# Reordering four engines' queues in a gated recurrent layer: `bw` before `yT`, `xc` before the last `M`, exponentials before squares, `ce` before `sqa`

## The chip, the core and the metric

One NeuronCore of a Trainium2 chip runs the whole kernel. Its engines are TensorE (PE in the profile, with its weight loads as PEld), VectorE (DVE), ScalarE (ACT), GpSimd (POOL) and SyncE (SP, which here issues DMAs). Each engine works through its own queue in order and waits on semaphores. The metric is the device time of one execution in microseconds, the median of several.

## The reference

The layer normalises u (4 sequences of 1024 tokens, 128 channels), runs a recurrent block with 32 heads, state 64 x 64 per head, and multiplies its output by a gate. Cut to what matters:

```python
proj = u @ in_proj_w.T                       # z, x, B, C, dt, theta, lambda
Bm = _rms(Braw, B_norm_w)[:, :, None, :] + B_bias
Cm = _rms(Craw, C_norm_w)[:, :, None, :] + C_bias
tc = jnp.cumsum(theta, axis=1)               # angles; rope() rotates B and C by them
Bm, Cm = rope(Bm), rope(Cm)
...
h = a_t * h + g_t * Bx + b_t * prevBx        # Bx = outer(x_t, B_t), scan over t
y = einsum('bhpn,bhn->bhp', h, C_t)
...
y = (y + xh * D) * silu(z)
y = _rms(y, norm_w)
return y @ out_proj_w.T
...
return x + s * silu(ffn(xn))                 # s: the block's output, ffn in emulated fp8
```

## The kernel before

A first part (`prepare`, about the first 145 us) normalises the input, transposes weights and stores tables to DRAM. The rest, `units`, is a loop over 8 super-tiles t of 512 tokens (four chunks of 128; two super-tiles make a sequence) and, inside, over 8 groups q of four heads: 64 units. The recurrence is done in chunks. In each chunk the outputs are a masked product of scores (C times B, in `s`) with decays (`E`), called `M`, applied to x (`xk`), plus the state (`hs`, `k_carry`) applied to decayed C (`ce`). There is no scheduler: every queue is in the order in which the code is written, and the queues are software-pipelined by hand. While a unit's outputs are formed, the next unit's B and C are rotated.

The names in one unit, with the engine that writes them:

- VectorE: `part` (L1299, eight of 128x512, products of B or C with rows of sines and cosines `k_trig`; both tensors are in SBUF), `ang` (L1274, angle subtraction), `hs` and `k_carry` (L1363, L1373, states), `xc` (L1283, two, x scaled for the skip, from PSUM), `M` (L1317, four, decay matrices from PSUM scores and `E`), `yT` (L1409, two, gated outputs, from PSUM), `bw` (L1309, two, B scaled by decays, from PSUM).
- GpSimd: `rot` (L1524, four, sum of two `part`), `ce` (L1533, two, decayed C), `sqa` (L1568, two, running sum of squares of the outputs over a super-tile; one, L1561, where q=0). All read and write SBUF.
- ScalarE: `E` (L1455, exponentials of `d`), `xk` (L1460, copies of x), `sz` (L1502), the sines `k_tri`, `sq` (L1465, squares of `yT`), and `rnd` (L1440, rounding for `ang`).
- TensorE: x products into `r` (L1112, `x_by_token`), whose result ScalarE copies and VectorE scales; transposes of rotated B into `r` (L1118), `d`, `s`, `y`, the output projection `o`, and at q=0 the column sums of `sqa` of the previous super-tile (L1164, `square_sums`), for the root mean square.
- SyncE copies the sines to both halves of the partitions (`k_trig`, eight DMAs a unit, L74) and loads the decay rows `eb` for `ce`, which it may overwrite once `ce` of the unit before is done.

Two waits matter at the places that the change touches. In TensorE's queue, at q=0, the sum of squares stands ahead of the x products of the next unit:

```python
                    exponents(t, q, 3)
                    if q == 0 and t > 0:
                        square_sums(t - 1)
                    if live(t, q + 1):
                        ...
                        x_by_token(t, q + 1, 0)
```

and it waits for the last `sqa` of the super-tile before (`pe.wait_ge(sqa_ready, at(T2, t, T2))`, L1162). In VectorE's queue each `xc` waits for ScalarE's copy of the same x (`x_copied`, L1279).

Of the kernel before, what the change touches and what calls it, by code (L numbers as in the profile page):

```python
# [36 lines left out]
NQ = H // 4  # L37
# [870 lines left out]
def units(nc, K, u, scratch, cum_stored, logs_stored, bc_loaded, xn_loaded, out):  # L908

    xn_d, tc_d, bc_d, cum_d, cumt_d, gate_d, logs_d, ecum_d = scratch  # L910
    with ExitStack() as ctx:
# [67 lines left out]
        def at(per, t, k):  # L979

            return t * per + max(k, 0) + 1
# [5 lines left out]
        def begins(t):  # L990

            return t % SPB == 0

        def ends(t):

            return t % SPB == SPB - 1
# [5 lines left out]
        def live(t, q):  # L1002

            return t * NQ + q < NS * NQ
# [260 lines left out]
        def _(dve):  # L1265
# [89 lines left out]
            for t in range(NS):  # L1355
                def state(t, q, c):

                    into = 1
                    if c == 0:
                        dve.wait_ge(y_ready, at(T2, t, 2 * q))  # L1360
                        dve.wait_ge(st_ready, at(T1, t, q + 1))
                        if begins(t):
                            nc.vector.tensor_copy(hs[:, 0, :, :].rearrange("n p d -> n (p d)"), R[1][:, 0:2 * HD]).then_inc(hch, 2)  # L1363
                            return
                    if c == CS - 1 and ends(t):
                        return
                    if c == CS - 2 and ends(t):
                        into = 2
                    dve.wait_ge(hch, at(T8, t, 8 * q + 2 * c))
                    for p in range(2):  # L1370
                        src = before(t, q, c, p)
                        dst = hs[:, c, p, :] if c < CS - 1 else K["carry"][:, t % 2, 2 * q + p, :]
                        nc.vector.scalar_tensor_tensor(  # L1373
                            out=dst, in0=src, scalar=K["dtot"][:, (t * CS + c) * NP + 2 * q + p:(t * CS + c) * NP + 2 * q + p + 1],
                            in1=R[1][:, (2 * c + p) * 64:(2 * c + p) * 64 + 64], op0=ALU.mult, op1=ALU.add).then_inc(hch, into)

                for q in range(NQ):
                    tn = t if q < NQ - 1 else t + 1
                    if live(t, q + 1):
                        rotation(t, q + 1, 0, 0, 0)  # L1380
                    if live(t, q + 2):
                        angles(t, q + 2)
                    for c in range(CS):
                        state(t, q, c)
                    if live(t, q + 1):
                        rotation(t, q + 1, 0, 0, 1)
                        x_scaled(t, q + 1, tn, 0)
                    scores(t, q, 2)
                    scores(t, q, 3)
                    if q == 0 and t > 0:  # L1390
                        norm_start(t - 1)
                    if live(t, q + 1):
                        x_scaled(t, q + 1, tn, 1)
                    if live(t, q + 1):
                        for p, w in ((1, 0), (0, 1), (1, 1)):
                            rotation(t, q + 1, p, w, 0)
                            rotation(t, q + 1, p, w, 1)
                            if q == 0 and t > 0:
                                if w == 0:
                                    norm_seeded(t - 1)  # L1400
                                else:
                                    norm_refined(t - 1, p)

                    for p in range(2):
                        dve.wait_ge(sz_ready, at(T2, t, 2 * q + p + 1))
                        dve.wait_ge(y_ready, at(T2, t, 2 * q + p + 1))
                        dve.wait_ge(out_ready, at(T1, t, q))
                        dve.wait_ge(sq_ready, at(T2, t, 2 * q))
                        nc.vector.tensor_tensor(yT[:, p, :], Yp[p][:], sz[:, p, :], ALU.mult).then_inc(yt_ready, 1)  # L1409
                    if q == 0 and t > 0:  # L1410
                        norm_refined(t - 1, 2)
                    if live(t, q + 1):
                        b_decayed(t, q + 1, tn)
                    if live(t, q + 1):
                        scores(t, q + 1, 0)
                        scores(t, q + 1, 1)
# [13 lines left out]
        def _(act):  # L1430
# [55 lines left out]
            for t in range(NS):  # L1486
                for q in range(NQ):
                    if live(t, q + 2):
                        rounding(t, q + 2)
                    decays(t, q, 2)  # L1490
                    decays(t, q, 3)
                    if q == 1 and t > 0:
                        normalised(t - 1)
                    if live(t, q + 1):
                        x_copy(t, q + 1, 0)
                        x_copy(t, q + 1, 1)
                    if q == 0 and t > 0:
                        root(t - 1)
                    for p in range(2):
                        act.wait_ge(z_ready, at(T2, t, 2 * q + p + 1))  # L1500
                        act.wait_ge(yt_ready, at(T2, t, 2 * q - 1 + p))
                        nc.scalar.activation(sz[:, p, :], R[p][:], ACT.Silu).then_inc(sz_ready, 1)  # L1502
                    if live(t, q + 2):
                        sines(t, q + 2)
                    if live(t, q + 1):
                        decays(t, q + 1, 0)
                    squares(t, q, 0)
                    if live(t, q + 1):
                        decays(t, q + 1, 1)
                    squares(t, q, 1)  # L1510
            root(NS - 1)
            normalised(NS - 1)
# [1 line left out]
        @block.gpsimd  # L1514
        def _(pool):
            for s in (rot_ready, ce_ready, sqa_ready):
                pool.sem_inc(s, 1)

            def sums(t, q, k):

                w, p = k // 2, k % 2
                pool.wait_ge(part_ready, at(T8, t, 8 * q + 2 * k + 2))
                pool.wait_ge(y_ready, at(T2, t, 2 * q - 2))
                nc.gpsimd.tensor_tensor(rot[:, q % 2, p, w, :], part[:, 2 * p, :], part[:, 2 * p + 1, :],  # L1524
                                        ALU.add).then_inc(rot_ready, 1)

            def c_decayed(t, q):

                pool.wait_ge(eb_loaded, 32 * (t * NQ + q + 1))
                for p in range(2):  # L1530
                    pool.wait_ge(rot_ready, at(T4, t, 4 * q + 4))
                    pool.wait_ge(y_ready, at(T2, t, 2 * q - 1 + p))
                    nc.gpsimd.tensor_tensor(ce[:, p, :], rot[:, q % 2, p, 1, :], eb[:, p, :], ALU.mult).then_inc(ce_ready, 1)  # L1533

            def gated_out(t):

                pool.wait_ge(acc_done, at(1, t, 1))
                pool.wait_ge(gate_loaded, 16 * (t + 1))
                nc.gpsimd.tensor_tensor(so[:], so[:], gate[:], ALU.mult).then_inc(gated, 1)

            def finished(t):

                pool.wait_ge(gated, t + 1)
                pool.wait_ge(res_loaded, 16 * (t + 1))
                nc.gpsimd.tensor_tensor(res[:], so[:], res[:], ALU.add).then_inc(o_ready, 1)

            for k in range(4):
                sums(0, 0, k)
            for t in range(NS):
                for q in range(NQ):  # L1550
                    c_decayed(t, q)
                    if live(t, q + 1):
                        for k in range(4):
                            sums(t, q + 1, k)
                            if k == 0 and q == 2 and t > 0:
                                gated_out(t - 1)
                            if k == 0 and q == 3 and t > 0:
                                finished(t - 1)
                    if q == 0:
                        pool.wait_ge(sq_ready, at(T2, t, 2))  # L1560
                        nc.gpsimd.tensor_tensor(sqa[:], sq[:, 0, :], sq[:, 1, :], ALU.add).then_inc(sqa_ready, 1)  # L1561
                        pool.wait_ge(sqa_ready, at(T2, t, 1))
                        pool.sem_inc(sqa_ready, 1)  # L1563
                        continue
                    for p in range(2):
                        pool.wait_ge(sq_ready, at(T2, t, 2 * q + p + 1))
                        pool.wait_ge(sqa_ready, at(T2, t, 2 * q + p))
                        nc.gpsimd.tensor_tensor(sqa[:], sqa[:], sq[:, p, :], ALU.add).then_inc(sqa_ready, 1)  # L1568
# [42 lines left out]
```

## Time and profile before

| | |
|---|---|
| median of 3 runs | 1208.13 us (1207.28 to 1209.54) |
| the profiled execution | 1207.62 us, span 1205.7 us |
| granted TensorE clock, mean | 0.971 |
| VectorE busy | 1144.0 us (95%) |
| TensorE busy | 1124.8 us (93%) |
| ScalarE busy | 819.0 us (68%) |
| GpSimd busy | 755.5 us (63%) |

Busy shares are of the span of the profiled execution. GpSimd's and ScalarE's rows leave room; VectorE's and TensorE's hardly do, though a TensorE that is shown busy needn't be at its peak. From about 150 us on the granted clock is in its top tenth.

### The profile page before, as it was taken

The numbers are of one execution on the slowest core, as the hardware profiler recorded it, in microseconds if no ns is written. First come the engines' busy times: TensorE is split into PE (matmuls) and PEld (weight loads), VectorE is DVE, ScalarE is ACT, GpSimd is POOL, SyncE is SP. The second block draws the span as 40 slices with busy tenths as digits, with TensorE's granted clock in tenths as the row PEclk, the third lists the DMA queues.
The fourth block names the chain that finished last, engine by engine and source line by source line (L and its number), as shares of the span: only waits on it lengthen the run. The fifth ranks groups of instructions, "written<-read, shape, count | busy, mean of one in ns | idle before, by whom it ended". The sixth has DMA issues, their size and how long they took to land.

```text
span 1205.7 us, 30426 instructions
## 1 busy us (share of the span) xinstructions
PE 1124.8 (93%) x11442; PEld 817.4 (68%) x11442; DVE 1144.0 (95%) x1821; ACT 819.0 (68%) x1270; POOL 755.5 (63%) x560
## 2 busy tenths in 40 slices
PE   3878399999999999999999999999999999999996
PEld 3663267777777767777776777776777777777775
DVE  7899599999999999999999999999999999999994
ACT  4678366677676677667667776667767767777663
POOL 5000247776776767666776677776767687667774
PEclk9976699999999999999999999999999999999999
DMA  8654555544645465546555464546444655444450
GB/s 180 219 148 104 124 113 119 113 106 103 144 106 125 103 142 117 118 98 137 116 124 107 94 148 112 122 104 152 105 116 99 136 117 128 107 90 98 113 118 16
DMA packets 91888, 142.94 MB, mean 119 GB/s; under 512 B 19326, under 2 KB 38591, under 8 KB 91327
## 3 DMA queue, kind: packets, MB, share of 16 engines
q1 hardware_dynamic: 91743, 141.00, 50.5%
q8 instruction: 91, 1.49, 0.6%
q14 instruction: 54, 0.44, 0.1%
HBM read 58.68 MB, written 13.37 MB: 60 GB/s over the span
## 4 chain that ended last, share of the span: by engine, by line
PE 59%; DVE 17%; issue 7%; DMA 2%; ACT 1%; SPq 1%; POOL 0%; DVEq 0%; POOLq 0%; ACTq 0%
PE y L1235 10%; PE r L1221 8%; PE s L1138 7%; PE o L1153 6%; PE r L1112 5%; PE y L1229 5%; PE r L1118 5%; PE y L1245 5%; DVE hs L1373 3%; DVE M L1317 3%; DVE bw L1309 3%; PE r L1107 3%; DVE xc L1283 3%; PE r L1193 3%; PE d L1127 3%
## 5 line engine op out<-in xcount | busy, mean ns | idle before, releaser
L1524 POOL TENSOR_TENSOR rot<-part 128x512 f32<-128x512 f32 x256 | 384.1, 1500 | 315.9 <-DVE part L1299 315.9
L1299 DVE SCALAR_TENSOR_TENSOR part<-k_bcs,k_prmT,k_trig 128x512 f32<-128x512 f32 x512 | 524.8, 1072 | 13.5 <-issue 9.7
L1455 ACT ACTIVATE E<-d 128x512 f32<-128x512 f32 x256 | 152.9, 597 | 184.5 <-PE d L1127 184.2
L1533 POOL TENSOR_TENSOR ce<-rot,eb 128x512 f32<-128x512 f32 x128 | 185.8, 1471 | 2.3 <-POOLq L1563 2.1
L1317 DVE TENSOR_TENSOR M<-s,E 128x512 f32<-128x512 f32 x256 | 163.3, 676 | 2.0 <-PE s L1138 1.6
L1568 POOL TENSOR_TENSOR sqa<-sqa,sq 128x512 f32<-128x512 f32 x112 | 142.7, 1274 | 31.3 <-ACT sq L1465 22.7
L1112 PE MATMUL r<-k_w_zx,k_xns 128*128 128x256 f32 x512 | 137.0, 391 | 13.6 <-issue 9.4
L1138 PE MATMUL s<-rot 64*128 64x128 f32 x2048 | 149.4, 286 | 0.0
L1138 PEld LDWEIGHTS s<-rot 64*128 64x128 f32 x2048 | 124.9, 188 | 35.2 <-issue 34.8
L1460 ACT COPY xk<-r 128x512 f32<-128x512 f32 x128 | 75.3, 588 | 106.8 <-PE r L1112 106.6
L1235 PE MATMUL y<-M,xk 128*64 128x128 f32 x2048 | 140.1, 279 | 0.0
L1153 PEld LDWEIGHTS o<-k_w_o,yT 128*128 128x128 f32 x1024 | 132.8, 192 | 8.5 <-DVE yT L1409 1.7
L1221 PE MATMUL r<-k_xns,k_w_zx 128*128 128x512 f32 x256 | 133.2, 614 | 3.8 <-DVE xc L1283 1.8
L1153 PE MATMUL o<-k_w_o,yT 128*128 128x128 f32 x1024 | 133.4, 275 | 1.4 <-DVE yT L1409 1.4
L1235 PEld LDWEIGHTS y<-M,xk 128*64 128x64 f32 x2048 | 109.2, 136 | 21.5 <-issue 21.5
L1112 PEld LDWEIGHTS r<-k_w_zx,k_xns 128*128 128x128 f32 x512 | 90.5, 192 | 31.9 <-issue 11.0
L1127 PE MATMUL d<-k_cum,k_pick 123*128 123x512 bf16 x256 | 99.4, 388 | 0.0
L1502 ACT ACTIVATE sz<-r 128x512 f32<-128x512 f32 x128 | 75.7, 597 | 32.7 <-PE r L1221 32.1
L1283 DVE TENSOR_TENSOR xc<-r,k_cc 128x512 f32<-128x512 f32 x128 | 87.0, 680 | 4.8 <-ACT xk L1460 4.7
L1193 PEld LDWEIGHTS r<-xk,bw 128*64 128x64 f32 x1792 | 57.5, 137 | 48.8 <-DVE bw L1309 48.0
L1229 PEld LDWEIGHTS y<-k_ident,xc 128*128 128x128 f32 x512 | 58.8, 140 | 44.7 <-issue 44.7
L1409 DVE TENSOR_TENSOR yT<-y,sz 128x512 f32<-128x512 f32 x128 | 81.6, 676 | 6.3 <-PE y L1245 6.3
(253 smaller groups left out, 1676.3 us busy)
## 6 DMA issues: line engine op xcount, KB each, us to landing
k_trig<-k_tri SPq DMA_DIRECT2D x512, 128.0 KB, 2.4
eb<-ecum_rows SPq DMA_DIRECT2D x128, 256.0 KB, 4.7
k_bcs<-bc_t SPq DMA_DIRECT2D x16, 256.0 KB, 4.1
k_bcs<-bc_t SPq DMA_DIRECT2D x32, 128.0 KB, 4.2
k_bcs<-in_L_attn_u SPq DMA_DIRECT2D x4, 512.0 KB, 6.1
xn_t<-a_xnT SPq DMA_DIRECT2D x1, 2048.0 KB, 11.5
tc_t<-a_tcT SPq DMA_DIRECT2D x1, 2048.0 KB, 15.9
bc_t<-a_tmp SPq DMA_DIRECT2D x1, 2048.0 KB, 8.5
```

Source lines behind the costliest of these rows:

```text
L1112: last = nc.tensor.matmul(R[i][:, 256 * c:256 * c + 256], xns[:, (t + q // NQ) % 2, (2 * i + c) * P:(2 * i + c + 1) * P], K["w_zx"][:, DI ...
L1127: nc.tensor.matmul(Dp[:], K["pick"][:, head * P:head * P + P], K["cum"][0:D_ROWS, q % 2, h, :], start=True, stop=True).then_inc(d_ready, 1)
L1138: last = nc.tensor.matmul(Sp[j][:, k], rot[rows, q % 2, p, 0, k], rot[rows, q % 2, p, 1, k], start=True, stop=True)
L1153: last = nc.tensor.matmul(Op[:, k], yT[:, p, k], K["w_o"][:, (2 * q + p) * P:(2 * q + p + 1) * P], start=False, stop=q == NQ - 1 and c == ...
L1221: nc.tensor.matmul(R[p][:], w, xns[:, t % 2, :], start=True, stop=True).then_inc(z_ready, 1)
L1235: nc.tensor.matmul(Yp[p][m:m + 64, k], xk[:, par, c, 128 * p + m:128 * p + m + 64], M[:, 2 * p + j, k], start=False, stop=c == 0 and begin ...
L1299: nc.vector.scalar_tensor_tensor(out=part[:, 2 * p + f, :], in0=bcs[:, (t + q // NQ) % 2, 2 * w + f, :], scalar=col, in1=trig[:, p, 1 - f, ...
L1317: nc.vector.tensor_tensor(M[:, h, :], Sp[h % 2][:], E[:, h % 2, :], ALU.mult).then_inc(m_ready, 1)
L1455: nc.scalar.activation(E[:, h % 2, :], Dp[:], ACT.Exp).then_inc(e_ready, 1)
L1524: nc.gpsimd.tensor_tensor(rot[:, q % 2, p, w, :], part[:, 2 * p, :], part[:, 2 * p + 1, :], ALU.add).then_inc(rot_ready, 1)
L1533: nc.gpsimd.tensor_tensor(ce[:, p, :], rot[:, q % 2, p, 1, :], eb[:, p, :], ALU.mult).then_inc(ce_ready, 1)
L1568: nc.gpsimd.tensor_tensor(sqa[:], sqa[:], sq[:, p, :], ALU.add).then_inc(sqa_ready, 1)
```

## The change

Four queues get another order; the instructions and their operands stay.

- VectorE scales B for the next unit (`bw`) ahead of the gated outputs `yT`, and the second `xc` ahead of the unit's last `M`.
- ScalarE computes the second exponential of the next unit ahead of the first of the two squares.
- GpSimd computes the decayed C of the next unit (`ce`) at the end of the iteration before, after its four `rot` and ahead of that iteration's `sqa`.

```diff
                     scores(t, q, 2)
-                    scores(t, q, 3)
                     if q == 0 and t > 0:
                         norm_start(t - 1)
                     if live(t, q + 1):
                         x_scaled(t, q + 1, tn, 1)
+                    scores(t, q, 3)
...
+                    if live(t, q + 1):
+                        b_decayed(t, q + 1, tn)
                     for p in range(2):
                         dve.wait_ge(sz_ready, at(T2, t, 2 * q + p + 1))
...
                     if q == 0 and t > 0:
                         norm_refined(t - 1, 2)
-                    if live(t, q + 1):
-                        b_decayed(t, q + 1, tn)
...
                         decays(t, q + 1, 0)
+                        decays(t, q + 1, 1)
                     squares(t, q, 0)
-                    if live(t, q + 1):
-                        decays(t, q + 1, 1)
                     squares(t, q, 1)
...
             for k in range(4):
                 sums(0, 0, k)
+            c_decayed(0, 0)
             for t in range(NS):
                 for q in range(NQ):
-                    c_decayed(t, q)
                     if live(t, q + 1):
                         for k in range(4):
                             sums(t, q + 1, k)
...
+                        c_decayed(*((t, q + 1) if q < NQ - 1 else (t + 1, 0)))
                     if q == 0:
```

GpSimd's queue from the end of one super-tile into the next. Before (`sqa` with one input, L1561, is the first of a super-tile, after its q=0):

```order
L1524 TENSOR_TENSOR rot<-part 128x512 x4
L1568 TENSOR_TENSOR sqa<-sqa,sq 128x512 x2
L1533 TENSOR_TENSOR ce<-rot,eb 128x512 x2
L1524 TENSOR_TENSOR rot<-part 128x512 x4
L1561 TENSOR_TENSOR sqa<-sq 128x512
```

and the same stretch of the changed kernel:

```order
L1523 TENSOR_TENSOR rot<-part 128x512 x4
L1532 TENSOR_TENSOR ce<-rot,eb 128x512 x2
L1568 TENSOR_TENSOR sqa<-sqa,sq 128x512 x2
L1523 TENSOR_TENSOR rot<-part 128x512 x4
L1532 TENSOR_TENSOR ce<-rot,eb 128x512 x2
L1561 TENSOR_TENSOR sqa<-sq 128x512
```

The pair of `ce` has moved ahead of the pair of `sqa`, for which TensorE waits at this place.

VectorE's queue from the second `part` of a unit with q=0 into the next unit (`nrm` and `tch` are small steps of the root mean square). Before:

```order
L1299 SCALAR_TENSOR_TENSOR part<-k_bcs,k_prmT,k_trig 128x512
L1283 TENSOR_TENSOR xc<-r,k_cc 128x512
L1317 TENSOR_TENSOR M<-s,E 128x512 x2
L1323 TENSOR_SCALAR nrm<-y 128x4
L1283 TENSOR_TENSOR xc<-r,k_cc 128x512
...
L1338 SCALAR_TENSOR_TENSOR tch<-tch,nrm 128x4
L1409 TENSOR_TENSOR yT<-y,sz 128x512 x2
L1342 SCALAR_TENSOR_TENSOR nrm<-tch,nrm 128x4
L1309 TENSOR_TENSOR bw<-r,k_dec 128x512 x2
L1317 TENSOR_TENSOR M<-s,E 128x512 x2
```

and in the changed kernel:

```order
L1299 SCALAR_TENSOR_TENSOR part<-k_bcs,k_prmT,k_trig 128x512
L1283 TENSOR_TENSOR xc<-r,k_cc 128x512
L1317 TENSOR_TENSOR M<-s,E 128x512
L1323 TENSOR_SCALAR nrm<-y 128x4
L1283 TENSOR_TENSOR xc<-r,k_cc 128x512
L1317 TENSOR_TENSOR M<-s,E 128x512
...
L1338 SCALAR_TENSOR_TENSOR tch<-tch,nrm 128x4
L1309 TENSOR_TENSOR bw<-r,k_dec 128x512 x2
L1411 TENSOR_TENSOR yT<-y,sz 128x512 x2
L1342 SCALAR_TENSOR_TENSOR nrm<-tch,nrm 128x4
L1317 TENSOR_TENSOR M<-s,E 128x512 x2
```

Of the four `M` of a unit the last one has moved behind the second `xc`, and the two `bw` ahead of the two `yT`.

## Rows read from the trace of the kernel before

**Rows 1.** The page, part 1: busy time of VectorE.
```profile
PE 1124.8 (93%) x11442; PEld 817.4 (68%) x11442; DVE 1144.0 (95%) x1821; ACT 819.0 (68%) x1270; POOL 755.5 (63%) x560
```

**Rows 2.** Sorted waits: engine and line, waited for, total us, times, longest.
```profile
POOL rot L1524 <- DVE part L1299: 315.9, 256, 41.7
...
PEld r L1221 <- DVE xc L1283: 50.5, 63, 1.5
...
DVE part L1299 <- DMA k_trig<-k_tri: 3.2, 9, 0.5
```

**Rows 3.** Timeline of VectorE, t=3 q=6: start us, duration us, engine, line.
```profile
641.07 1.27 DVE L1409 TENSOR_TENSOR yT<-y,sz 128x512 f32<-128x512 f32 x2
642.27 1.27 DVE L1309 TENSOR_TENSOR bw<-r,k_dec 128x512 f32<-128x512 f32 x2
...
644.66 1.46 DVE L1299 SCALAR_TENSOR_TENSOR part<-k_bcs,k_prmT,k_trig 128x512 f32<-128x512 f32 x1
...
648.11 0.93 DVE L1299 SCALAR_TENSOR_TENSOR part<-k_bcs,k_prmT,k_trig 128x512 f32<-128x512 f32 x1
...
650.76 0.67 DVE L1283 TENSOR_TENSOR xc<-r,k_cc 128x512 f32<-128x512 f32 x1
651.36 6.09 DVE L1299 SCALAR_TENSOR_TENSOR part<-k_bcs,k_prmT,k_trig 128x512 f32<-128x512 f32 x6
```

**Rows 4.** Timeline of GpSimd in the same unit.
```profile
641.23 1.27 POOL L1524 TENSOR_TENSOR rot<-part 128x512 f32<-128x512 f32 x1 [0.63 <-DVE part L1299]
...
642.89 2.69 POOL L1568 TENSOR_TENSOR sqa<-sqa,sq 128x512 f32<-128x512 f32 x2 [0.39 <-ACT sq L1465]
...
645.54 2.96 POOL L1533 TENSOR_TENSOR ce<-rot,eb 128x512 f32<-128x512 f32 x2
```

**Rows 5.** Timeline of TensorE and ScalarE in the same unit.
```profile
646.78 1.13 PE L1112 MATMUL r<-k_w_zx,k_xns 128*128 128x256 f32 x4
...
649.70 0.59 ACT L1460 COPY xk<-r 128x512 f32<-128x512 f32 x1 [1.17 <-PE r L1112]
...
656.65 1.09 PE L1118 MATMUL r<-k_ident,rot 128*128 128x128 f32 x8
```

**Rows 6.** Timeline of VectorE in an even super-tile, t=4 q=6.
```profile
771.93 1.27 DVE L1409 TENSOR_TENSOR yT<-y,sz 128x512 f32<-128x512 f32 x2
...
779.00 0.75 DVE L1299 SCALAR_TENSOR_TENSOR part<-k_bcs,k_prmT,k_trig 128x512 f32<-128x512 f32 x1
...
782.06 6.10 DVE L1299 SCALAR_TENSOR_TENSOR part<-k_bcs,k_prmT,k_trig 128x512 f32<-128x512 f32 x6
```

**Rows 7.** Timeline of the boundary units, t=4 q=0, then t=5 q=0.
```profile
673.67 1.27 DVE L1409 TENSOR_TENSOR yT<-y,sz 128x512 f32<-128x512 f32 x2
...
679.38 0.95 PE L1164 MATMUL y<-k_ones,sqa 128*128 128x1 f32 x8
...
804.24 1.27 DVE L1409 TENSOR_TENSOR yT<-y,sz 128x512 f32<-128x512 f32 x2
...
809.71 0.95 PE L1164 MATMUL y<-k_ones,sqa 128*128 128x1 f32 x8
...
812.29 0.69 DVE L1283 TENSOR_TENSOR xc<-r,k_cc 128x512 f32<-128x512 f32 x1 [0.30 <-ACT xk L1460]
...
813.43 0.59 ACT L1460 COPY xk<-r 128x512 f32<-128x512 f32 x1 [1.17 <-PE r L1112]
...
814.76 1.40 DVE L1299 SCALAR_TENSOR_TENSOR part<-k_bcs,k_prmT,k_trig 128x512 f32<-128x512 f32 x2
```

**Rows 8.** Timeline of VectorE, t=4 q=1, then t=5 q=1.
```profile
690.66 1.27 DVE L1409 TENSOR_TENSOR yT<-y,sz 128x512 f32<-128x512 f32 x2
...
701.21 6.10 DVE L1299 SCALAR_TENSOR_TENSOR part<-k_bcs,k_prmT,k_trig 128x512 f32<-128x512 f32 x6
...
820.99 1.27 DVE L1409 TENSOR_TENSOR yT<-y,sz 128x512 f32<-128x512 f32 x2
...
831.31 6.10 DVE L1299 SCALAR_TENSOR_TENSOR part<-k_bcs,k_prmT,k_trig 128x512 f32<-128x512 f32 x6
```

## The prediction, made before the changed kernel had run

> **What bounds the kernel now.** I read the page first: VectorE is busy for 1144.0 of 1205.7 us [rows 1]. The sorted waits come next. Their largest entries are other engines waiting for VectorE: GpSimd waits 315.9 us for rotation products, and TensorE's loads wait 50.5 us for `xc` [rows 2]. VectorE itself has almost no idle time, so in the main loop the time is VectorE's time, and only what shortens or interrupts its row counts.
>
> Then the timeline of one ordinary unit (t=3, q=6). I count offsets from its first gated output `yT`, 641.07 in the trace. VectorE has two `yT` and two `bw` (0.60 apart each), two `M`, the first `part` at 3.59, the angle subtraction, the states, the second `part` at 7.04, `xc`, two `M`, `xc` at 9.69, and six `part` from 10.29 that end at 16.38 [rows 3]. Every row starts 0.08 before its predecessor's end, so the unit is 16.30 long. Its counterpart in an even super-tile has the six products at 10.13 and is 16.15 long [rows 6].
>
> The reader should look at how long `part` takes. It reads two SBUF tensors, as every GpSimd addition and product here does. Six take 6.09 us, yet the second one of the even unit takes 0.75 [rows 3, 6]. The first one of the ordinary unit takes 1.46. It starts at 3.59 while GpSimd's pair of `sqa` runs from 1.82 to 4.51, and it ends at 5.05, 0.54 after the pair [rows 3, 4]. The second takes 0.93 and ends at 7.97, 0.54 after GpSimd's `ce` pair (7.43). GpSimd waits likewise: its `ce` pair takes 2.96, against 2.50 for two products of 1.27 overlapped by 0.04. So the two engines exclude each other for whole instructions, and at a hand-over the waiting VectorE product goes first. An `M`, `yT`, `bw` or `xc` with one input in PSUM isn't lengthened. What remains of VectorE's loss in the first 10 us of a unit is thus the placing of two `part` against GpSimd's two pairs.
>
> [...]
>
> **The change, part by part.** No instruction is added or removed on any engine; each keeps its duration.
>
> *`bw` ahead of `yT`.* Swapping two pairs of equal length moves nothing behind them on VectorE. `bw` needs the transposes of B, which run on TensorE from 656.65 to 657.74, while VectorE would ask for the first at 657.37 and the second at 657.97 [rows 5]. The first four of eight transposes are done by then, so there's no wait now, with some 0.1 to spare, and more where TensorE runs ahead. Cost 0. `yT` comes 1.20 later. Who waits: ScalarE's squares, now also behind the second exponential (below).
>
> *Exponential ahead of squares.* ScalarE's squares end about 0.6 later; their reader `sqa` stands behind `ce` now, so this is hidden. The cover is `ce`, which ends at 4.07, against squares done near 3.2. The rounding behind them ends near 3.9, before the angle subtraction wants it at 4.54. Cost 0.
>
> *`ce` ahead of `sqa`.* The last `rot` ends at 1.43 [rows 4]. `ce` follows 0.14 later (the gap inside the dependent `sqa` pair: 2.69 less two times 1.27 is 0.15) and ends at 1.57 + 2.50 = 4.07. The first `part` starts at 3.59 as before, is blocked to 4.07 and ends at 4.62 rather than 5.05: 0.43 won. The `sqa` pair comes behind it. In the rows before, a pair ends 2.38 after the product that held it (645.54 + 2.96 against 644.66 + 1.46), and the dependence adds 0.18: 4.62 + 2.56 = 7.17. The second `part` starts 1.99 after the first's end, at 6.61, inside this pair, and ends at 7.17 + 0.54 = 7.72 rather than 7.97. So 0.25 is left of the 0.43. In an even unit the second `part` starts at 7.07 at the latest, also before 7.17, and ends at 7.72 rather than 7.82: 0.10 [rows 6].
>
> *`xc` ahead of the last `M`.* VectorE would start the second `xc` at 7.72 - 0.08 + 1.20 = 8.84 instead of 9.69. It needs ScalarE's copy, which ends at 9.22 now; that chain starts with TensorE's x product at 5.71, released by the angle subtraction [rows 5]. Released 0.43 earlier, the copy ends at 8.79: just in time, by 0.05. TensorE gets `xc` earlier, but TensorE isn't the bound. Gain 0, bounds 0 and 0.4 lost per unit.
>
> An ordinary unit thus loses 0.25 (odd t) or 0.10 (even t). There are 19 and 20 of q = 3 to 7: 19 x 0.25 + 20 x 0.10 = 6.8 us won. Lower bound 0 (the copy late by what was won), upper bound 0.43 each, 17 us.
>
> *The boundary between super-tiles.* At q=0, t>0 TensorE's sum of squares (L1164) waits for the last `sqa` of the previous super-tile, and everything behind it on TensorE's queue waits too: both x products, then the copies, both `xc`. Now it starts at 809.71, 5.47 into the unit (5.71 in an even one), long after `sqa`'s end [rows 7]. Afterwards `sqa` ends at 7.17, so it starts at 7.27 (0.1 for the signal, estimated from the 0.08 between a `part` end and its `rot`). That is 1.80 (1.56) later. From there the second copy ends 4.31 later (813.43 + 0.59), `xc` at 4.34. Before, the six products came at 5.05 after the sums, since both `M` had filled the wait; now the last `M` stands behind `xc`, so they come 4.34 + 0.60 + 0.60 = 5.54 after. Cost of a boundary: 1.80 + 0.49 = 2.29 (odd), 2.05 (even); 4 x 2.29 + 3 x 2.05 = 15.3 us over seven.
>
> *The two units after it.* In q=1 there is a single `sqa`, which ends near 5.7, so the second `part` isn't blocked; TensorE starts its scores 0.4 earlier and the copies come near 7.5 and 8.4. The six products start at about 9.93, not 10.32 (odd) or 10.55 (even) [rows 8]: 4 x 0.39 + 3 x 0.62 = 3.4 us won. In q=2 TensorE is late after a short q=1, and `bw` waits up to 0.4 for its transposes; I take no change there (bounds 0.5 won, 0.9 lost).
>
> **Sum.** +15.3 - 3.4 - 6.8 = +5.1 us. The profiled execution took 1207.62 us (span 1205.7 and 1.9 around it), 0.5 under the median of 1208.13. So 1212.7 us, 0.38% above the median. What a measurement of this kernel can tell from no change is about 0.2%, 2.4 us.
>
> **Rivals.** *No change to be measured.* The ordinary units save 0.1 more each, by TensorE's lead over its `bw` and `xc` waits: 46 units, 4.6 us, 1208. Against it: VectorE has no wait in those rows that this lead could shorten.
>
> *Faster.* The sum of squares isn't held. If GpSimd got through `sqa` by 5.5, the seven boundaries would cost nothing and 10.2 us stay won: 1197.4. The point is 10.2 / 7 = 1.46 per boundary; below it the change gains. For it: `sqa` is only 2.7 us of work. Against: the `ce` pair alone fills GpSimd to 4.07, and even with the first `part` not in between `sqa` would end at 6.7, 1.2 too late.
>
> *Slower still.* The first `part` arrives after 4.03 instead of 3.59. Then `sqa` takes over directly from `ce`, and `part` waits until 5.3 and ends near 5.9; a unit loses about 0.9 instead of winning. What could delay it: a late `bw` in q=2, or the trig rows, whose landing already holds `part` nine times, by up to 0.5 us [rows 2]. Seven to fifteen such units give 1219 to 1226.
>
> **How the numbers follow.** My forecast 0.60 (own range 1209 to 1217), no change 0.17, faster 0.13, slower still 0.10. The range reaches to 1203, into the faster case, and to 1219, and leaves out what lies beyond 1219 and below 1203, about 2 in 10. A part of the forecast's range lies under 1210.5. So: faster by over 0.2% 0.17, within 0.19, slower 0.64.
>
> **What would show it.** Right: the L1164 sums start near 7.3 into their unit and VectorE's first `xc` there waits about 2 us, seven times; in an ordinary unit the first `part` takes about 1.0 and the second about 1.1, and the unit is 16.05; `sqa` runs from 4.6 to 7.2. Wrong: boundary units of 17 us; or first products of 1.5 us and more; or waits of VectorE for the transposes or for the copies (`bw`, `xc`) in ordinary units, which would mean that TensorE, not the exclusion, sets the new period.

## The result and the profile after

The changed kernel takes 1235.2 us (median, 1234.1 to 1235.62), the kernel before 1208.31 in the same comparison: a ratio of 1.0207, 95% interval 1.018 to 1.0233. The profiled execution took 1234.1 us, 26.5 more than that of before. The sign was forecast, the size wasn't: 1212.7 was predicted, with 1219 as the upper end.

The page of the kernel after, busy time of each engine and the granted clock in 40 slices:

```profile
PE 1120.3 (91%) x11442; PEld 830.5 (67%) x11442; DVE 1144.4 (93%) x1821; ACT 814.2 (66%) x1270; POOL 755.1 (61%) x560
...
PEclk9976699999999999998999999999999999999999
```

VectorE's busy time is the same as in [rows 1] to 0.4 us, and a product that GpSimd holds up counts as busy, so nearly all of the 26.5 us is idle time on VectorE. The sorted waits say where (engine and line, waited for, total us, times, longest):

```profile
DVE xc L1283 <- ACT xk L1460: 31.3, 20, 4.0
...
PE y L1164 <- POOL sqa L1568: 15.5, 8, 2.1
...
DVE bw L1309 <- PE r L1118: 5.5, 9, 2.6
```

The reader should see that two of the three rows belong together. TensorE waits 15.5 us for `sqa`, at most 2.1 us at a time (seven boundaries and once after the last unit), and VectorE then waits 31.3 us for the x copies, up to 4.0 us at a time. A wait of 2.1 has become one of 4.0 further down.

An ordinary unit, t=3 q=6, the same as in [rows 3 to 5] (timeline: start us, duration us, engine, line):

```profile
652.98 1.28 DVE L1309 TENSOR_TENSOR bw<-r,k_dec 128x512 f32<-128x512 f32 x2
...
654.54 2.52 POOL L1532 TENSOR_TENSOR ce<-rot,eb 128x512 f32<-128x512 f32 x2
...
656.57 1.03 DVE L1299 SCALAR_TENSOR_TENSOR part<-k_bcs,k_prmT,k_trig 128x512 f32<-128x512 f32 x1
...
657.01 3.14 POOL L1568 TENSOR_TENSOR sqa<-sqa,sq 128x512 f32<-128x512 f32 x2
...
659.59 1.11 DVE L1299 SCALAR_TENSOR_TENSOR part<-k_bcs,k_prmT,k_trig 128x512 f32<-128x512 f32 x1
...
661.18 0.59 ACT L1460 COPY xk<-r 128x512 f32<-128x512 f32 x1 [1.17 <-PE r L1112]
...
661.82 0.68 DVE L1283 TENSOR_TENSOR xc<-r,k_cc 128x512 f32<-128x512 f32 x1
...
663.02 6.09 DVE L1299 SCALAR_TENSOR_TENSOR part<-k_bcs,k_prmT,k_trig 128x512 f32<-128x512 f32 x6
```

It goes as worked out. The first `part` starts at 3.59 and takes 1.03 instead of 1.46, the second takes 1.11 inside `sqa`, the copy ends 0.05 before `xc` starts, and the six products come at 10.04. The unit is 16.05 long.

The boundary of t=5 (`yT` of this unit follows `bw` at 819.14, so offsets count from there), as in [rows 7]:

```profile
826.44 1.02 PE L1164 MATMUL y<-k_ones,sqa 128*128 128x1 f32 x8 [2.09 <-POOL sqa L1568]
...
827.33 1.31 PE L1112 MATMUL r<-k_w_zx,k_xns 128*128 128x256 f32 x4
828.43 1.92 PE L1153 MATMUL o<-k_w_o,yT 128*128 128x128 f32 x8
...
829.29 0.69 DVE L1283 TENSOR_TENSOR xc<-r,k_cc 128x512 f32<-128x512 f32 x1 [2.45 <-ACT xk L1460]
...
830.14 1.71 PE L1112 MATMUL r<-k_w_zx,k_xns 128*128 128x256 f32 x4
...
832.51 0.69 DVE L1283 TENSOR_TENSOR xc<-r,k_cc 128x512 f32<-128x512 f32 x1 [1.85 <-ACT xk L1460]
...
833.71 1.41 DVE L1299 SCALAR_TENSOR_TENSOR part<-k_bcs,k_prmT,k_trig 128x512 f32<-128x512 f32 x2
```

The sums start at 7.30, where 7.27 was forecast. But the second four x matmuls take 1.71 and the projection between them 1.92; at the boundary of t=4 and in the ordinary unit the same instructions take 1.03 and 1.05. Three stretches behind the start of the sums of this boundary (start, end and length of the stretch; then busy us and instruction count of PE, PEld, DVE, ACT and POOL; the third figure from the end is the granted clock):

```profile
826.40:828.10 1.70, 1.66 (x12) 1.61 (x13) 0.44 (x1) 0.00 (x0) 1.18 (x1) 1.00 0.53 157
828.10:831.52 3.42, 3.42 (x14) 3.06 (x13) 1.36 (x3) 0.59 (x1) 0.09 (x1) 0.50 0.00 1
831.52:833.50 1.98, 1.98 (x13) 1.47 (x12) 0.99 (x2) 1.59 (x2) 0.00 (x0) 1.00 0.00 0
```

TensorE had been idle for 2.09 us before the sums, and behind them its granted clock is 0.50 for 3.4 us: 1.2 GHz instead of 2.4. The boundary of t=4 had the same wait and kept its clock:

```profile
692.40:694.10 1.70, 1.65 (x12) 1.60 (x13) 0.45 (x1) 0.00 (x0) 1.17 (x1) 1.00 0.94 165
694.10:697.50 3.40, 3.40 (x24) 2.90 (x22) 2.00 (x5) 1.83 (x3) 0.10 (x1) 1.00 0.04 9
...
694.28 1.05 PE L1153 MATMUL o<-k_w_o,yT 128*128 128x128 f32 x8
695.17 1.03 PE L1112 MATMUL r<-k_w_zx,k_xns 128*128 128x256 f32 x4
```

In 3.4 us of the same queue it gets through 24 matmul instructions there, against 14 above.

Measured from the end of one unit's eighth `part` to the next, and summed by q over both traces, the difference is this:

| units | before, us | after, us | difference | forecast |
|---|---|---|---|---|
| boundaries, q=0 of t=1 to 7 | 117.45 | 144.54 | +27.1 | +15.3 |
| q=1 of t=1 to 7 | 115.61 | 117.05 | +1.4 | -3.4 |
| q=2, all t | 132.11 | 136.10 | +4.0 | 0 |
| q=3 to 7, 39 units | 632.46 | 626.92 | -5.5 | -6.8 |

The boundary of t=4, with the full clock, took 19.08 us, the six others, each with a stretch at 0.50, 20.5 to 22.1.

### The profile page after: what moved, and what is told of

Read it like the earlier page. It is cut to its first block and busy times, and to the rows that moved or that the text cites. A ratio compares the mean times of both kernels' runs of the same rounds, so it can differ in the third digit from the quotient of the medians.

```text
span 1232.2 us, 30426 instructions
## 1 busy us (share of the span) xinstructions
PE 1120.3 (91%) x11442; PEld 830.5 (67%) x11442; DVE 1144.4 (93%) x1821; ACT 814.2 (66%) x1270; POOL 755.1 (61%) x560
## 5 line engine op out<-in xcount | busy, mean ns | idle before, releaser
L1568 POOL TENSOR_TENSOR sqa<-sqa,sq 128x512 f32<-128x512 f32 x112 | 165.7, 1480 | 15.6 <-ACT sq L1465 7.6
L1317 DVE TENSOR_TENSOR M<-s,E 128x512 f32<-128x512 f32 x256 | 168.4, 677 | 1.8 <-PE s L1138 1.5
L1532 POOL TENSOR_TENSOR ce<-rot,eb 128x512 f32<-128x512 f32 x128 | 161.1, 1281 | 8.5
L1112 PE MATMUL r<-k_w_zx,k_xns 128*128 128x256 f32 x512 | 145.4, 409 | 22.9 <-issue 9.3
L1138 PE MATMUL s<-rot 64*128 64x128 f32 x2048 | 149.3, 285 | 16.9 <-DVE M L1317 16.9
L1153 PEld LDWEIGHTS o<-k_w_o,yT 128*128 128x128 f32 x1024 | 138.1, 198 | 9.2 <-DVE yT L1411 1.7
L1153 PE MATMUL o<-k_w_o,yT 128*128 128x128 f32 x1024 | 138.4, 281 | 1.4 <-DVE yT L1411 1.4
L1221 PE MATMUL r<-k_xns,k_w_zx 128*128 128x512 f32 x256 | 121.1, 594 | 0.5 <-DVE xc L1283 0.4
L1283 DVE TENSOR_TENSOR xc<-r,k_cc 128x512 f32<-128x512 f32 x128 | 87.3, 682 | 31.5 <-ACT xk L1460 31.3
L1502 ACT ACTIVATE sz<-r 128x512 f32<-128x512 f32 x128 | 75.7, 597 | 17.3 <-PE r L1221 11.5
## 6 DMA issues: line engine op xcount, KB each, us to landing
tc_t<-a_tcT SPq DMA_DIRECT2D x1, 2048.0 KB, 16.3
```

The source lines that it names most:

```text
L1112: last = nc.tensor.matmul(R[i][:, 256 * c:256 * c + 256], xns[:, (t + q // NQ) % 2, (2 * i + c) * P:(2 * i + c + 1) * P], K["w_zx"][:, DI ...
L1138: last = nc.tensor.matmul(Sp[j][:, k], rot[rows, q % 2, p, 0, k], rot[rows, q % 2, p, 1, k], start=True, stop=True)
L1153: last = nc.tensor.matmul(Op[:, k], yT[:, p, k], K["w_o"][:, (2 * q + p) * P:(2 * q + p + 1) * P], start=False, stop=q == NQ - 1 and c == ...
L1221: nc.tensor.matmul(R[p][:], w, xns[:, t % 2, :], start=True, stop=True).then_inc(z_ready, 1)
L1317: nc.vector.tensor_tensor(M[:, h, :], Sp[h % 2][:], E[:, h % 2, :], ALU.mult).then_inc(m_ready, 1)
```

## The experiments

The quoted text in each part is what was expected before its run. The unit times below are measured in the same way, each in one profiled execution. Ratios are to the kernel before in the same comparison. In the traces of the experiments the stage ahead of the loop took about 147 us or, in three of them, about 154; the kernel before, whose times there lie near 1208 and near 1215, seems to do the same. This widens the medians by some 6 us. The unit times don't contain it, and neither does the time of the loop, which is given in places: from the end of the first eight `part` to the last instruction, 1058.3 us before and 1085.0 in the changed kernel.

### Keeping TensorE busy during the wait

```diff
                 pe.wait_ge(yt_ready, at(T2, t, T2))
+                if t < NS - 1:
+                    for _ in range(8):
+                        nc.tensor.matmul(Yp[0][:], K["zeros_bf"][0:MASK_ROWS, :], K["cum"][0:MASK_ROWS, 0, 0, :], start=True, stop=True)
                 pe.wait_ge(sqa_ready, at(T2, t, T2))
```

> The changed kernel with eight extra matmuls of zeros into the free bank Yp[0] ahead of TensorE's wait for the last sqa at seven boundaries; the wait itself stays. Theory (the idle 2.1 us drops TensorE's granted clock to half and stretches the x products behind it): boundary units fall from 20.7 to about 19.1 us, no half-clock stretch behind the sums, total about 1223 us. Rival (the stretch after the sums has another cause, and the clock is only a companion): total within 2 us of the changed kernel's 1235.

Ratio 1.0109 (1.0061 to 1.0157), median 1227.11 us, against 1223 expected. The profiled execution, 1218.95, is the shortest of four (the others take 1226.46 to 1231.3), so what follows is shown for that one. Timeline of the boundary of t=5, with the eight extra matmuls in its first row:

```profile
815.99 1.89 PE L1164 MATMUL y<-k_cum,k_zeros_bf 85*128 85x512 bf16 x8
818.16 1.05 PE L1167 MATMUL y<-k_ones,sqa 128*128 128x1 f32 x8 [0.28 <-POOL sqa L1571]
...
820.91 1.03 PE L1112 MATMUL r<-k_w_zx,k_xns 128*128 128x256 f32 x4
```

and the stretch behind its sums (columns as above):

```profile
820.00:823.40 3.40, 3.40 (x23) 2.80 (x22) 2.16 (x5) 1.99 (x3) 0.00 (x1) 1.00 0.00 0
```

The sums come hardly earlier in the unit (818.16 is 7.21 after `bw`), `xc` still waits 2.19 us, and matmuls whose result nobody reads make the kernel faster, since the clock stays at 1.00. What is left of TensorE's wait is 0.28 us. The boundaries took 18.84 to 19.03 us, 132.9 in all: 11.6 less than in the changed kernel and 15.5 more than before, where the prediction had 15.3. So the wait and its price were right, and the clock was what it lacked. The Trainium skill (TensorE: Matmul & The Clock Gate, Part 1) says that the array has two clock levels and falls to 1.2 GHz when idle. The traces show the two levels, but not so simply: 0.50 behind the wait of 2.09 us at t=5, 1.00 behind that of 2.10 at t=4, and 1.00 behind 0.1 to 0.3 here.

### Old order on GpSimd at the boundary, and in two units more

In the first, `ce` goes ahead of `sqa` at q < 7 only, in the second at q = 2 to 6 only; elsewhere `sqa` comes first again. The diff is the first's; the second has `1 < q < NQ - 1` in both places:

```diff
-                        c_decayed(*((t, q + 1) if q < NQ - 1 else (t + 1, 0)))
+                        if q < NQ - 1:
+                            c_decayed(*((t, q + 1) if q < NQ - 1 else (t + 1, 0)))
...
+                    if live(t, q + 1) and not (q < NQ - 1):
+                        c_decayed(*((t, q + 1) if q < NQ - 1 else (t + 1, 0)))
```

> The changed kernel with GpSimd's old order (sqa pair ahead of ce) at q=7 alone, so that the sum of squares at the boundary isn't held by ce. Theory: the sums start near 5.8 us into their unit, TensorE's clock stays full, a boundary costs 0.8 us rather than 3.9, total 1213 to 1215 us. Rival (the boundary's cost comes from bw and xc moved on VectorE): the boundary units stay over 18.5 us and the total over 1222 us.

> The changed kernel with GpSimd's old order at q=7, 0 and 1; ce ahead of sqa at q=2 to 6 alone. Theory (in the units q=1 and q=2 the first part comes just when ce ends, and sqa takes the ports from under it for 1.2 us): those units fall to 16.3 to 16.6 us, total 1207 to 1210 us. Rival (those units are slow because bw waits for TensorE): as the kernel with the old order at q=7 alone, within 2 us.

The first: ratio 1.0074 (1.0047 to 1.0101), median 1220.01, above the 1213 to 1215 expected. Four boundaries take 17.49 to 17.62 us, 0.7 to 0.8 over before as expected; three take 19.13 to 19.32, and these again have the low clock. A short wait is enough for it (timeline of t=3):

```profile
549.90 1.02 PE L1164 MATMUL y<-k_ones,sqa 128*128 128x1 f32 x8 [0.51 <-POOL sqa L1569]
550.78 2.03 PE L1112 MATMUL r<-k_w_zx,k_xns 128*128 128x256 f32 x4
```

The stretch behind it:

```profile
551.00:554.20 3.20, 3.20 (x12) 2.84 (x13) 1.25 (x3) 0.59 (x1) 2.88 (x2) 0.50 0.02 4
```

So "the clock stays full" was too much: it stayed full at four of seven.

The second: ratio 1.0064 (1.0034 to 1.0094), median 1221.68, where 1207 to 1210 was expected. Its q=1 units are at 16.34 to 16.49 as expected, but seven of its eight q=2 units at 17.86, which neither theory had. In the one of t=4 `bw` waits 0.35 us for its transposes, and GpSimd waits 2.19 us for the squares and starts `sqa` at 3.54. So GpSimd, with `ce` last, is late with `rot` and then with its extra product `so` of that unit, which the six `part` run into:

```profile
726.59 3.02 POOL L1532 TENSOR_TENSOR ce<-rot,eb 128x512 f32<-128x512 f32 x2
...
730.80 1.27 POOL L1538 TENSOR_TENSOR so<-so,gate 128x512 f32<-128x512 f32 x1
730.90 7.08 DVE L1299 SCALAR_TENSOR_TENSOR part<-k_bcs,k_prmT,k_trig 128x512 f32<-128x512 f32 x6
```

The six take 7.08 instead of 6.09. The order that suits one unit hurts another.

### `ce` ahead of `sqa` alone: at q=7, at q=2 to 6, at every q

All three are the kernel before, with VectorE's and ScalarE's queues untouched. The diff is the first's; the second has `1 < q < NQ - 1` as its condition, the third none:

```diff
+            c_decayed(0, 0)
             for t in range(NS):
                 for q in range(NQ):
-                    c_decayed(t, q)
...
+                        if q == NQ - 1:
+                            c_decayed(*((t, q + 1) if q < NQ - 1 else (t + 1, 0)))
...
+                    if live(t, q + 1) and not (q == NQ - 1):
+                        c_decayed(*((t, q + 1) if q < NQ - 1 else (t + 1, 0)))
```

> The kernel before with one thing changed: ce ahead of the sqa pair at q=7 alone; VectorE's and ScalarE's queues as before. Theory (wait of 1.8 us plus a half-clock stretch worth 1.7 us or more, seven times): total 1230 to 1234 us, though only seven pairs of products have moved. Rival (my prediction's price, the wait alone): 1208 + 7 x 1.7 = 1220 us.

> The kernel before with one thing changed: ce ahead of the sqa pair at q=2 to 6. VectorE's and ScalarE's queues as before. Theory (the ordinary units' gain is GpSimd's order alone; bw, xc and the exponential give nothing): units q=3 to 7 at 16.05 to 16.1 us, boundaries and q=1 and q=2 as before, 5.6 us saved, ratio 0.995. Rival (the gain needs bw ahead of yT, so that TensorE is early): those units stay at 16.15 and 16.30, no difference.

> The kernel before with ce ahead of the sqa pair at every q, VectorE's and ScalarE's queues as before. Theory: boundaries 18.5 us, 20.1 with a half-clock stretch (0.5 less than in the changed kernel, since both M fill the wait for xc), q=1 units near 16.1 since the small nrm step isn't blocked by ce any more, ordinary units 16.05; total 1220 to 1228 us. Rival (VectorE's new order is what costs in q=1 and q=2 and at the boundary): total under 1218 us. Other rival (it costs nothing): 1233 to 1236 us.

At q=7 alone: ratio 1.0135 (1.0105 to 1.0166), median 1229.5 us. Moving one pair of GpSimd products past another at seven places costs 16 us by the ratio, and 20.3 at the boundaries of the profiled execution. Three boundaries take 18.6 us, three 20.13 to 20.15, and one, with the low clock for 6.8 us, 21.50. The first are 1.7 to 1.9 above before, the wait alone. The median lies just under the theory's 1230 to 1234 and well above the rival's 1220; but the low clock came at four boundaries of seven, not at all seven.

At q=2 to 6 alone: ratio 0.9979 (0.9958 to 1.0001). The interval just reaches 1, but the trace decides: units q=4 to 7 take 16.05 us (a few 16.14), q=3 16.12 to 16.21 but for 16.06 in t=0, and boundaries, q=1 and q=2 are as before. The 39 units from q=3 on take 626.9 us, 5.6 less than before, and as much as in the changed kernel. GpSimd's order alone gives all of the ordinary units' gain.

At every q: ratio 1.0186 (1.0152 to 1.0219), median 1231.96, above what was expected. Boundaries take 18.6 us with the full clock and 19.9 to 20.15 without, as expected; four of seven had the low clock. q=1 stays at 16.41 to 16.66, as before, at t=1 to 6 (16.91 at t=7), where I had expected 16.1: TensorE isn't early enough for its copies, and the first `xc` waits 0.61 us for one at t=4. Six q=2 units take 16.12 to 16.14, where the changed kernel needs up to 17.3; the two others take 17.17 and 16.99, and three ordinary units 16.91 to 17.19. The intervals of this kernel and of the changed one overlap, so by their totals `ce` ahead everywhere may be the whole slowdown. In the two profiled executions the loop takes 1073.6 us here and 1085.0 in the changed kernel; the boundaries are 8.4 longer there and q=2 is 5.2 longer, while the ordinary units are 2.6 shorter.

### VectorE's and ScalarE's moves alone

The changed kernel with GpSimd's queue as before.

> The changed kernel with GpSimd's old order everywhere: VectorE's and ScalarE's moves alone. By the exclusion of part and GpSimd's pairs, worked out as in the prediction: the sqa pair is split by the first part (3.8 to 4.4), the second part gets in between the two ce, the six products start near 9.8, an ordinary unit takes 15.85 us; boundaries start their sums near 5.6, so no low clock there; total 1195 to 1203 us. Rival (bw, xc and the exponential give nothing, the gain was ce's place): ordinary units 16.15 to 16.30, total 1207 to 1210 us.

Ratio 1.0105 (1.0062 to 1.0148), median 1219.72. This kernel loses as well, without any move on GpSimd. Timeline of t=4 q=6:

```profile
778.71 1.28 DVE L1309 TENSOR_TENSOR bw<-r,k_dec 128x512 f32<-128x512 f32 x2
...
781.33 2.95 POOL L1569 TENSOR_TENSOR sqa<-sqa,sq 128x512 f32<-128x512 f32 x2 [1.19 <-ACT sq L1465]
782.30 0.84 DVE L1299 SCALAR_TENSOR_TENSOR part<-k_bcs,k_prmT,k_trig 128x512 f32<-128x512 f32 x1
784.23 3.03 POOL L1532 TENSOR_TENSOR ce<-rot,eb 128x512 f32<-128x512 f32 x2
785.38 0.75 DVE L1299 SCALAR_TENSOR_TENSOR part<-k_bcs,k_prmT,k_trig 128x512 f32<-128x512 f32 x1
...
788.55 6.08 DVE L1299 SCALAR_TENSOR_TENSOR part<-k_bcs,k_prmT,k_trig 128x512 f32<-128x512 f32 x6
```

The unit is 15.85 long, exactly as worked out and shorter than with the whole change. The later squares have shifted `sqa` so that the first `part` waits only for the rest of its first addition, and the second `part` isn't held at all. But the total was missed by 17 us or more: from t=1 on q=2 takes 17.8 to 17.9 and q=3 16.8 to 16.9, the units where GpSimd's extra products stand, and the boundaries take 17.5 to 17.7, once 19.25 with the low clock that I had ruled out. Over q=3 to 7 the 39 units take 626.9 us, the same 5.6 less than before that `ce` ahead gives by itself, and the whole change gives no more: the two gains don't add up.

### `xc` behind both `M` again

```diff
                     scores(t, q, 2)
+                    scores(t, q, 3)
                     if q == 0 and t > 0:
                         norm_start(t - 1)
                     if live(t, q + 1):
                         x_scaled(t, q + 1, tn, 1)
-                    scores(t, q, 3)
```

> The changed kernel with the second xc behind both M again. Theory: boundaries 0.5 us shorter than in the changed kernel at the same clock, all other units within 0.05 us of it; total 3 to 4 us under the changed kernel. Rival (xc ahead of M serves TensorE): ordinary units 0.1 us or more longer, total not below the changed kernel.

Ratio 1.0138 (1.0102 to 1.0174). The boundaries with the full clock take 18.59 to 18.65 us, against 19.0 to 19.08 with `xc` ahead: 0.4 to 0.5 less, where 0.49 was worked out. Units q=4 to 7 stay at 16.05, but for one of 16.31 and two of 17.17 and 16.92, in which the first `part` was held by the landing of the trig rows (VectorE idle for 0.46 and 0.33 us), as my slower rival had it. The median, 1225.58, is 10 us below the changed kernel's, more than the 3 to 4 that I had expected. The profiled loop is 12.7 us shorter than the changed kernel's. Only some 3.4 of that are what `xc` costs (0.49 at seven boundaries). The low clock came at four boundaries instead of six, and most q=1 and q=2 units took 16.1 to 16.3, 6.7 us less in all, which the theory of this move doesn't explain.

### The small `nrm` step out of the way of `ce`

```diff
                     if live(t, q + 1):
                         b_decayed(t, q + 1, tn)
+                    if q == 0 and t > 0:
+                        norm_refined(t - 1, 2)
                     for p in range(2):
...
-                    if q == 0 and t > 0:
-                        norm_refined(t - 1, 2)
```

> The changed kernel with the last small nrm step of q=0 ahead of yT instead of behind it. Theory (this step reads two SBUF tensors, is held by ce for 0.2 us, and so puts the first part of the next unit at the moment when ce ends, where sqa may win): its first part starts near 3.7 instead of 3.9, waits for ce and then goes ahead of sqa, so every q=1 unit takes 16.0 to 16.2 us (now 16.2 or 17.0 to 17.25); total 3 to 6 us under the changed kernel. Rival (TensorE or the trig rows are late there): q=1 units over 16.9 us remain.

This is about the units q=1. In the changed kernel (timeline of t=4 q=1):

```profile
705.79 2.51 POOL L1532 TENSOR_TENSOR ce<-rot,eb 128x512 f32<-128x512 f32 x2
...
706.69 0.40 DVE L1342 SCALAR_TENSOR_TENSOR nrm<-tch,nrm 128x4 f32<-128x4 f32 x1
...
708.22 1.86 DVE L1299 SCALAR_TENSOR_TENSOR part<-k_bcs,k_prmT,k_trig 128x512 f32<-128x512 f32 x1
708.26 1.27 POOL L1561 TENSOR_TENSOR sqa<-sq 128x512 f32<-128x512 f32 x1
```

The step of four elements a partition takes 0.40, held by `ce`. That puts the first `part` at 708.22, in the last 0.08 us of `ce`; `sqa` goes first and `part` takes 1.86. With the step ahead of `yT` (t=5 q=1 of the experiment):

```profile
842.47 0.18 DVE L1342 SCALAR_TENSOR_TENSOR nrm<-tch,nrm 128x4 f32<-128x4 f32 x1
842.76 2.51 POOL L1532 TENSOR_TENSOR ce<-rot,eb 128x512 f32<-128x512 f32 x2
844.96 0.86 DVE L1299 SCALAR_TENSOR_TENSOR part<-k_bcs,k_prmT,k_trig 128x512 f32<-128x512 f32 x1
845.23 1.72 POOL L1561 TENSOR_TENSOR sqa<-sq 128x512 f32<-128x512 f32 x1
```

The `part` comes 0.31 before `ce` ends, waits and goes first. All seven q=1 units behind a boundary take 15.97 to 16.02, where the prediction had 16.02 for them. The total went the other way, 1239.12 us, ratio 1.0253 (1.0215 to 1.0292): all boundaries had the low clock this time, three of them for 6.8 us instead of 3.4, and every q=2 unit took 17.3, two more than in the changed kernel. The expectation for the total failed, that for the units held.

### A version chosen unit by unit

Old order everywhere at the boundary, in q=1 and q=2; `ce` ahead only at the end of q=2; `bw` and the second exponential ahead at the end of q=3 to 6, `xc` ahead in q=4 to 7. The diff is against the kernel before. The lines shown stand ahead of `yT`, of the squares and of `sqa` in turn; with the opposite condition each call stands in its old place:

```diff
-                    scores(t, q, 3)
+                    if q < 4:
+                        scores(t, q, 3)
...
+                    if q >= 4:
+                        scores(t, q, 3)
...
+                    if 2 < q < NQ - 1:
+                        b_decayed(t, q + 1, tn)
...
+                    if 2 < q < NQ - 1:
+                        decays(t, q + 1, 1)
...
+                        if q == 2:
+                            c_decayed(*((t, q + 1) if q < NQ - 1 else (t + 1, 0)))
```

> A version chosen unit by unit: ce ahead of sqa at the end of q=2 alone; bw ahead of yT and the second exponential ahead of the squares at the end of q=3 to 6, xc ahead of the last M in q=4 to 7; everything else as before, so that the boundary, q=1 and q=2 keep the old order. Theory: units q=4 to 7 at 15.85 to 16.0 us as in the kernel with VectorE's and ScalarE's moves alone, q=3 at 16.13, the rest as before: 10 us saved, about 1198 us, ratio 0.992. Rival (what is won there is lost when the old order resumes at the boundary): 1205 us or more.

Ratio 0.9959 (0.9937 to 0.9981), median 1204.12: faster than both kernels, by 5.8 us against before in the same comparison and not by 10. Units q=5 to 7 take 15.77 to 16.02 (one 17.27), q=3 16.05 to 16.20. But q=4, the first with the new order at its head, takes 16.17 to 16.41; I had it at 15.85 to 16.0. The boundary units keep 16.67 to 16.92. It isn't shown to be better than `ce` ahead at q=2 to 6 alone, which is simpler: the intervals overlap, and the loop takes 1053.6 us here and 1053.4 there.

## Why the prediction was wrong

- *VectorE sets the time, and `part` against GpSimd's pairs is what varies.* Right. The ordinary units, before, after and in the experiments, follow the durations in [rows 3] and [rows 4].
- *`ce` ahead of `sqa` in an ordinary unit.* Right: 1.03 and 1.11 for the two products, 16.05 for the unit, 5.5 us won against 6.8. I had used 0.25 and 0.10 for all, and q=3, q=4 and q=7 won less, some of them next to nothing. That GpSimd's order is enough for it was shown by moving only that.
- *`bw` ahead of `yT` costs 0; the exponential and `xc` cost 0.* Right in ordinary units together with `ce`'s move, where removing `xc`'s changed nothing; the exponential and `bw` weren't moved alone. That together they shift `sqa` into a better place when `ce` stays behind, 15.85, I had not seen.
- *The boundary, 2.29 and 2.05 each.* This step failed in what it left out. What it held was right: sums at 7.30 for 7.27, the first `xc` waiting 2.25 at the full clock where about 2 was forecast, and 15.5 us for seven boundaries against 15.3 once TensorE was kept busy. But a wait on TensorE has a second price, the granted clock behind it. Six of seven boundaries had a stretch at 0.50, which cost 1.4 to 3 us each over the boundary with the full clock. The boundaries together took 11.6 us more than with TensorE kept busy, more than half of the miss. The prediction put this at nothing and never asked what the clock does behind a wait, though the trace of before shows it at the head of the loop (timeline, then a stretch with the columns as above):

```profile
148.88 1.97 PE L1118 MATMUL r<-k_ident,rot 128*128 128x128 f32 x8 [6.39 <-POOL rot L1524]
...
148.88:152.60 3.72, 3.72 (x21) 3.10 (x23) 1.38 (x2) 0.60 (x1) 2.49 (x2) 0.50 0.69 151
```

  Behind a wait of 6.39 us, and already in its last 3 us, the clock is at 0.50, and the eight transposes take 1.97 us instead of the 1.09 in [rows 5]. What that trace couldn't show is that waits of 0.5 to 2.1 us can bring it too: from there on TensorE waits for at most 0.67 us at a time before the end of the loop, and its clock is full.
- *q=1, 3.4 us won; q=2, no change.* This step failed too: 1.4 and 4.0 lost. The mechanism is the one that I had as the slower rival: the first `part` comes when `ce` ends, `sqa` goes first. I had put the point at 4.03 after the unit's start and given it a chance of 0.10. The edge lies about 0.1 before `ce` ends, not 0.04. What I missed in q=1 is that the `nrm` step reads two SBUF tensors and is itself held by `ce`, 0.2 us, and moving it brought all seven units to the forecast 16.0. In q=2 `bw` did wait, 0.2 to 0.35 at t=4 and 5, and that moved `part` to the edge. Two q=2 units of the same trace show the two sides, t=4 and then t=5, both starting from the end of the eighth `part` (721.55 and 856.15):

```profile
721.89 1.29 DVE L1309 TENSOR_TENSOR bw<-r,k_dec 128x512 f32<-128x512 f32 x2 [0.34 <-PE r L1118]
...
725.49 1.85 DVE L1299 SCALAR_TENSOR_TENSOR part<-k_bcs,k_prmT,k_trig 128x512 f32<-128x512 f32 x1
725.52 2.96 POOL L1568 TENSOR_TENSOR sqa<-sqa,sq 128x512 f32<-128x512 f32 x2
...
856.36 1.29 DVE L1309 TENSOR_TENSOR bw<-r,k_dec 128x512 f32<-128x512 f32 x2 [0.21 <-PE r L1118]
...
859.96 0.74 DVE L1299 SCALAR_TENSOR_TENSOR part<-k_bcs,k_prmT,k_trig 128x512 f32<-128x512 f32 x1
860.11 3.15 POOL L1568 TENSOR_TENSOR sqa<-sqa,sq 128x512 f32<-128x512 f32 x2
```

The `part` at 3.94 takes 1.85 and the unit 17.29; the `part` at 3.81 takes 0.74 and the unit 16.20. Their `ce` pairs end at 725.57 and 860.14, so the one `part` comes 0.08 and the other 0.18 before. A difference of 0.13 us in `bw`'s wait becomes 1.1 us. With `bw` behind `yT` again, in the experiment with `ce` ahead at every q, six of the eight q=2 units take 16.12 to 16.14.

- *The faster rival and the one of no change.* Both fell with the boundary. With GpSimd's order restored at q=7 the ratio was still 1.0074.

The difference of 21.4 us between the forecast 1212.7 and the profiled 1234.1 is 11.6 of clock, 4.8 in q=1, 4.0 in q=2, 1.3 in the ordinary units: 21.7.

What stays open is why the same wait lowers the clock at one boundary and not at the next. Over the traces of all kernels with a wait of TensorE for `sqa`, the clock fell at 25 of 35 boundaries with waits of 1.4 to 2.1 us, at 6 of 21 with waits of 0.5 to 0.7, and at none of the seven with 0.1 to 0.3. It fell behind none of TensorE's 135 other waits of 0.5 to 1.4 us in these loops. The runs don't show what makes the difference. That q=4 of the chosen version is 0.3 to 0.5 longer than worked out wasn't followed up either.

## What to carry to other kernels

Price a new wait on TensorE twice: its own length, and what the matmuls behind it cost at half the clock. Where the wait can't be avoided, idle matmuls into a free bank ahead of it may give more back than they take. Where two engines exclude each other, write down for each instruction with two SBUF inputs when it arrives against the other engine's pair; one that arrives about 0.1 us before a hand-over can go either way, and even a step of four elements counts. And a reordering in a periodic loop should be judged by kind of unit: here the same change won up to 0.26 us in each of 39 units and lost 2 to 5 in each of seven.

## What the hardware showed that was not expected

- Behind an idle time of TensorE of 0.50 to 2.1 us its granted clock was 0.50 for 3.4 us or for 6.8 us. TensorE was busy again from the start of that stretch in all but two of the 31 cases, where the stretch began 0.7 and 0.3 us before the wait ended. Behind the same idle time elsewhere the clock was 1.00.
- At a hand-over a waiting VectorE product went ahead of GpSimd's next one each time that it had been issued 0.12 us or more before the end of the one that held it, 729 times in the twelve traces; at less than 0.08 it came too late in 16 of 19 cases, and in between it went either way. The Trainium skill (SBUF — State Buffer, "Who interferes with whom") says that a VectorE instruction with two SBUF inputs contends with a GpSimd instruction that reads SBUF, and, for VectorE's 2-port modes, that whoever issues first gets the shared pair and the other blocks fully. The trace agrees with the full blocking for two SBUF inputs, and shows in addition that "first" is decided slightly before the end of the instruction in progress.
